# Second attention: output projections and turned maxima in 128x32 column tiles, and the maxima one score chunk earlier in steps with pair sums

## The reference

```
x = conv_attention(x)                     # 1x1 convolutions, softmax over 1024x1024, residual, relu
t = tokens(x)
t = t + attention(layernorm(t))           # 8 heads of 32, the "second attention"
t = t + experts(layernorm(t))             # 8 experts, the best 2 of each token
```

```
qkv = x @ w_qkv
dots = einsum('bhid,bhjd->bhij', q, k) * dim ** -0.5
attn = softmax(dots, axis=-1)
out = einsum('bhij,bhjd->bhid', attn, v)  # then (b, n, 256)
return out @ w_out + b_out
```

## Time and profile before

| what | value |
|---|---|
| three runs | 1159.1, 1163.66, 1166.8 us |
| profiled execution, own time | 1163.12 us |
| its span in the trace | 1161.3 us |
| TensorE clock granted, mean | 0.984 |
| busy: PE, PEld | 1087.0 us (94%), 737.8 us (64%) |
| busy: DVE, ACT, POOL | 816.4, 629.6, 594.3 us |

### The profile page before, as it was taken

The page is one execution under the profiler, slowest core; times in us unless marked ns, Lnnn a source line. Parts: engine busy times, 40 slices in busy tenths (PEclk is TensorE's granted clock), DMA queues, the critical chain, the costliest instruction groups (busy, mean ns, idle before and its releaser), DMA issues.

```text
span 1161.3 us, 34638 instructions
## 1 busy us (share of the span) xinstructions
PE 1087.0 (94%) x13440; PEld 737.8 (64%) x13440; DVE 816.4 (70%) x1489; ACT 629.6 (54%) x1144; POOL 594.3 (51%) x510
## 2 busy tenths in 40 slices
PE   7999998979899998999999989899999999999996
PEld 4464555435455555555555545688898998999884
DVE  4666666666788889788888982777565566565773
ACT  3566675645677667766775665453233333333332
POOL 3425241324588763876487456177554554453530
PEclk9999999998899999999999999999999999999997
DMA  5245851724323231533253213824332332332328
GB/s 177 91 161 202 329 173 60 236 73 154 93 63 94 75 87 35 122 85 103 70 119 93 62 46 101 309 39 92 57 47 47 57 47 48 56 44 41 47 39 294
DMA packets 98908, 121.00 MB, mean 104 GB/s; under 512 B 29024, under 2 KB 76064, under 8 KB 98112
## 3 DMA queue, kind: packets, MB, share of 16 engines
q1 hardware_dynamic: 75280, 70.40, 20.8%
q0 software_dynamic: 20400, 42.08, 15.8%
q10 hardware_dynamic: 3072, 6.30, 1.5%
HBM read 73.10 MB, written 45.47 MB: 102 GB/s over the span
## 4 chain that ended last, share of the span: by engine, by line
PE 70%; DVE 16%; issue 5%; DMA 3%; ACT 2%; DVEq 2%; POOL 1%; SPq 0%; ACTq 0%; POOLq 0%
PE PP L1022 23%; PE PP L1449 13%; DVE mxp L1740 9%; PE PP L1334 7%; PE PP L1306 6%; PE PP L1193 4%; PE PP L1121 4%; PE PP L1253 3%; PE PP L1038 3%; PE PP L1316 2%; PE PP L1321 2%; PE PP L1153 1%; PE PP L1408 1%; DMA res_d<-WORK,lb 1%; DVEq L2019 1%
## 5 line engine op out<-in xcount | busy, mean ns | idle before, releaser
L954 ACT ACTIVATE WB<-PP 128x512 f32<-128x512 f32 x512 | 265.3, 605 | 111.9 <-PE PP L1334 110.7
L1740 DVE TENSOR_REDUCE mxp<-PP 128x2 f32<-128x1024 f32 x242 | 287.0, 1219 | 51.3 <-PE PP L1253 50.7
L992 ACT ACTIVATE WORK<-PP,b1c 128x256 f32<-128x256 f32 (+1 forms) x320 | 139.2, 450 | 234.7 <-PE PP L1022 193.2
L698 POOL TENSOR_TENSOR WB<-WB 128x1024 f32<-128x1024 f32 x81 | 191.7, 2368 | 82.2 <-PE PP L1321 49.6
L781 POOL DMA_INDIRECT res_d<-WORK,lb x70 | 117.1, 1673 | 153.6 <-DVE WORK L2037 136.5
L1449 PE MATMUL PP<-WB,WORK 128*128 x1704 | 193.0, 273 | 0.0
L1022 PE MATMUL PP<-WORK,WB 128*128 128x256 f16 (+1 forms) x1552 | 175.8, 273 | 2.4 <-DVE WORK L2006 1.7
L1449 PEld LDWEIGHTS PP<-WB,WORK 128*128 128x128 f16 x1704 | 164.8, 98 | 19.2 <-issue 0.2
L1022 PE MATMUL PP<-WORK 128*128 128x128 f16 (+6 forms) x1086 | 162.7, 301 | 10.9 <-DVE WORK L1657 3.6
L1022 PEld LDWEIGHTS PP<-WORK,WB 128*128 (+1 forms) x1552 | 152.5, 102 | 21.6 <-issue 4.5
L1334 PE MATMUL PP<-WORK 97*32 97x256 f16 x4096 | 160.0, 276 | 5.0 <-ACT WB L954 4.5
(11 more groups left out here) (318 smaller groups left out, 1197.3 us busy)
## 6 DMA issues: line engine op xcount, KB each, us to landing
WORK<-in_L_ffn_W_dram POOLq DMA_DIRECT2D x32, 512.0 KB, 4.1
res_d<-WORK SPq DMA_DIRECT2D x8, 1024.0 KB, 4.5
late_d<-WB POOLq DMA_DIRECT2D x1, 6144.0 KB, 19.1
WB<-late_d ACTq DMA_DIRECT2D x3, 2048.0 KB, 12.9
v_d<-WORK SPq DMA_DIRECT2D x4, 1024.0 KB, 5.7
WORK<-q_hi_d SPq DMA_DIRECT2D x16, 256.0 KB, 4.0
WORK<-v_d SPq DMA_DIRECT2D x8, 512.0 KB, 5.5
WORK<-k_hi_d SPq DMA_DIRECT2D x16, 256.0 KB, 4.4
```

The source lines that it names most:

```text
L698: pool.tensor_tensor(PS[n % 2], PR[n % 3][:, 0], PR[n % 3][:, 1], ALU.add).then_inc(s("pair_kept"), 1)
L954: act.activation(PR[n % 3][:, c // 2, c % 2 * 2:c % 2 * 2 + 2], SCORES[m % 3] .rearrange("p (h n) -> p h n", h=2), ACT.Exp).then_inc(s("e_ ...
L992: act.activation(hid[:, k, 0:width], hidden_bank(k)[:, 0:width], ACT.Gelu, bias=b1c[:, bass.ds(e, 1), k], scale=1.0 / WSCALE)\
L1740: dve.tensor_reduce(mxp[:, n // 4 % 2, i, h:h + 2, k], PP[2 + h // 2][:, :].rearrange("p (h n) -> p h n", h=2), X_AXIS, ALU.max).then_inc( ...
```

## The change

Three edits. `max_row` uses a plain matmul against the identity where it used a transpose. `tail_project` cuts each of its two products into four, one for every 32 tokens, with the output on the 32 partitions of that tile; it has 8 matmuls of 264 columns where it had 2. In `attend`, a step with pair sums puts the maximum group behind two chunks where it stood behind three; a step with direct sums stays as it was.

```
-                pe.transpose(bank[0:2 * GH, 0:P], mx[:, :], identf[:, :]).then_inc(s("c_made"), 1)
+                pe.matmul(bank[0:2 * GH, 0:P], mx[:, :], identf[:, :], start=True, stop=True).then_inc(s("c_made"), 1)
...
-                tok_at = slice(t * P, (t + 1) * P)
-                product(bank[:, 0:WIDE], [(OS[:, k, tok_at], wo_sb[:, k]) for k in range(CC)], "c_made")
+                for k in range(CC):
+                    for r in range(P // D):
+                        mm = pe.matmul(bank[r * D:(r + 1) * D, 0:WIDE], OS[:, k, t * P + r * D:t * P + (r + 1) * D],
+                                       wo_sb[:, k], start=(k == 0), stop=(k == CC - 1), skip_group_check=True)
+                mm.then_inc(s("c_made"), 1)
...
-                    for c in range(3):
+                    ahead = 3 if direct(n - LAG) else 2
+                    for c in range(ahead):
...
-                    score_chunk(n, 3)
+                    for c in range(ahead, 4):
+                        score_chunk(n, c)
```

## The result

| | before | after |
|---|---|---|
| median of 22 runs each, us | 1162.35 (1158.66 to 1167.68) | 1165.57 (1161.26 to 1169.98) |
| ratio, 95% interval | | 1.0026, 1.0015 to 1.0036 |
| profiled execution, own time, us | 1163.12 | 1164.63 |
| its span, us | 1161.3 | 1162.3 |
| granted clock, mean over the runs | 0.9865 (35 runs beside the first set of experiments) | 0.9825 |

The change costs 3.2 us, and the interval leaves no doubt of the sign. The forecast was 1159.0 (1153 to 1164): wrong in sign and outside the range. It was counted from 1163.66, the median of three runs of before; counted from the 1162.35 of 22 runs, the same 4.7 us would have given 1157.7.

The account below looks back on a forecast made before the run. PE bounds projection steps and DVE's reductions plain pair-sum steps of the second attention. Savings of 1.7 (held group) + 1.8 (last six projections) + 0.7 (turned rows) + 0.5 (transitions) = 4.7 us, from 1163.66 to 1159.0, range 1153 to 1164.

Parts of the forecast that it names:

- The projection in tiles: Second attention: projection falls from 1.08 to 0.89 us, pair sum ahead from 0.54 to 0.43; PE's work 0.30 less per projection.
- Plain steps: Pair-sum steps without a projection, bound by DVE's reductions: stay at 2.86 us from group to group wherever the group stands.
- the group was held: Rival that the group isn't held by DVE: 24 projections save 0.30 us each, 1153.5 us in all; chance 0.14.
- the turned rows do not cost 0.80: Rival that float32 matmul streams 128 columns four times: eight rows lose 4.9 us, 1163.9 us in all; chance 0.04.
- The held group's step: 24 projection steps in batches 1 to 3: PE waits 0.30 us for DVE, step 3.81 against 3.88, saving 1.7 us.
- slower by the held group: Rival that PE waits more than 0.37 us at the group, lengthening projection steps: 1164 to 1167 us; chance 0.06.
- Turned rows: Rows behind direct sums in batches 1 to 3: 0.09 us saved per step, eight times, 0.7 us.
- Behind direct sums [...] PE is the bound: Steps 21, 25, 29 of batches 1 and 2, 21 and 25 of batch 3: PE's time counts, so 0.09 us each.
- Transitions: Where direct sums give way to pair sums, a chunk less between groups: 0.15 us in batches 1 and 2, 0.5 together.
- Six last projections: End of the last batch and behind it, where no groups are left: the full 0.30 us each, 1.8 us.
- next to nothing: Rival that the wait eats the 0.07 and a transfer the end's 1.8 us: 1.2 us remain, 1162.5; chance 0.14.
- The last two: Projections within the first expert tile, between 128x128 products: eight groups of 0.22 plus two switches of 0.11, no change.

Follow-up runs that it names:

- f3: After with the row turned by a transpose again instead of the plain matmul: 1164.12 us, 1.0021 of before.
- h1: Before with only the two projections inside the first expert tile in tiles: 1164.66 us, 1.0014 of before.
- g1: After with three chunks ahead of every maximum group and the last batch's eight projections 128x128 again: 1158.53 us, 0.9967 of before.
- g2: After with three chunks ahead of every maximum group and only the last three projections 128x128 again: 1153.54 us (6 runs), 0.9918 of before.
- h3: The kernel of g2 measured again, in a second set of runs: 1154.44 us (7 runs), 0.9936 of before.
- g4: After with three chunks ahead of the group in the 24 steps behind a projection, two in other pair-sum steps: 1162.63 us, 1.0006 of before.
- e1: After with three chunks ahead of the maximum group in every step, tiles and plain-matmul rows kept: 1159.74 us, 0.9971 of before.

## Why the prediction was wrong, point by point

**Right.** The projection in tiles costs 0.89 us and the pair sum ahead of it 0.43, 0.11 less than ahead of the 128x128 form. These 0.11 us agree with the Trainium skill (TensorEngine Tiling (Array Packing), Key Properties), which says that a change of the tiling mode drains the TensorE; as a rule alone it would have given 0.2 per projection, and 0.30 came. DVE holds the group in all 24 steps. Plain steps stay at 2.86. The transitions out of direct sums gave 0.22 (batch 0) and 0.24 (group 30 of batch 2, forecast 0.24 with its row). Of the rivals, the group was held (so not 1153), and the turned rows do not cost 0.80: two records of 0.27 us lie beside score records, and f3 with a transpose takes the same time. The Trainium skill (TensorE: Matmul & The Clock Gate, Terms) calls float32 four times faster in transpose mode; as time this is not seen here, where the way from the sums to the group is 1.84 us with the plain matmul and 1.94 with the transpose (f3). (Worked out from its own terms, this rival would have cost 8 x (0.80 - 0.22) = 4.6 us and not 4.9.)

**The held group's step: mis-sized, 1.7 forecast, 0.06 measured.** Two small errors lie in it. The group starts 0.89 behind the first chunk and not 0.85: L1785 starts 0.08 behind the end of the last projection record, where before it started 0.04 behind it. (The ends of matmuls are modelled, so that the 0.04 may as well lie in the model.) That made 3.81 into 3.855, 24 x 0.045 = 1.1 us. And 3.88 was taken for all 24 steps of before, from one step in the middle of a run. The first of each run, nine in all, took 3.82: the group ahead of it had waited for DVE and cost 0.33. That is 9 x 0.06 = 0.5 us. The wait's own size was right (24 x 0.28 = 6.8 us).

The rival "slower by the held group" set its limit at 0.37 us of wait. The wait was 0.34 by that count (0.89 - 0.55), so the step stayed just on the winning side.

**Turned rows: 0.7 forecast, about 0.2.** The failed step is "Behind direct sums [...] PE is the bound". Chunk 3 waits there 0.29 us for an exponential, before as after, and takes the 0.11 back. Only the two rows ahead of group 30 paid, and they share their 0.24 with the moved group.

**Transitions: 0.5 forecast, about 0.3.** They gave 0.22 and twice 0.13; missed was group 14, three times 0.05 us longer.

**Six last projections: 1.8 forecast, 0.9 arrived.** The failed step is in the rival "next to nothing": the 1.35 us of idle PE ahead of the turned tokens was looked at as a possible transfer, at 0.14, and dropped. It is a chain of register loads of fixed length, which starts only when PE's sequencer has handed over the matmuls ahead of it. Time won in front of such a chain is won only so far as the sequencer gets there sooner as well.

**The last two "come to about what they cost now: nothing"**, and nothing else behind the hand-over was thought to move. That was the large miss: with tiles the part behind the hand-over is 2.5 to 4.4 us longer. 2 us of it is the clock in both traces of after (0.5 in others), which falls behind a longer idle of PE (2.19 us for 1.35). Most of the rest seems to hang on just the two projections that were booked at nothing (h1: 2.1 us, with an interval that just touches none); by what mechanism is open.

**Sum, from the traces:** 0.06 + 0.2 + 0.3 + 0.9 = 1.5 us won in the attention (1.1 between the traces of before and after; two traces of before differ by 0.7), less 2.5 to 4.4 behind it: 1.0 to 2.9 us slower. The medians say 3.2.

**Open.** Why g1, with all eight whole, is 4 to 5 us above g2 and h3, where the five tiled projections should bring about 1.5; the traces of g1 and g2 themselves (1156.86 and 1157.09 us) don't show the difference. Whether the clock falls at the hand-over seems a matter of chance with a slant: with 2.1 to 2.2 us of idle PE in five traces of six, with 1.2 to 1.4 in two of nine. And what share of the second half the projection right ahead of the loads has, and what share the two behind them.

## What to carry to other kernels

Before a group of work is moved ahead of other work, ask who sets its earliest start. Where another engine sets it and PE is otherwise the bound, each piece that is moved behind it adds its full length (0.22 us here, 24 times), and a cheaper piece ahead of it brings nothing until it has been moved back: do the tiles, leave the order. Take the length of a step from every kind of neighbour it has, not from one in mid-run. And look at what the sequencer has to do behind the last matmul: more and shorter matmuls can cost the lead that hid its register loads. The best version here is three chunks throughout with all projections but the last three in tiles: 1153.5 and 1154.4 us, 0.992 and 0.994 of before.

## What the runs showed of the hardware

- A register load on PE's sequencer follows the one before it at 0.65 us (the second at 0.9 to 1.0), and five with what follows them make 3.6 to 3.7 us in 15 traces. What PE still has to do when they begin hides them only in part: PE idles 1.2 to 1.4 or 2.1 to 2.2 us behind it.
- A float32 product in four 128x32 tiles streams as weighing does (0.22 us for four records of 264 columns), but its result is seen later: DVE starts 0.25 us behind the next matmul's start, 0.11 for the 128x128 form.
- The two float32 records of 8 output rows seem to block one column tile only: three records of the next line start at the same instant as the first of them (462.91).
- The clock fell to its lower level for 3.4 or 6.8 us behind an idle PE of about 2.2 us at the hand-over, at a price of 0.5 and 2.0 us (in g1 and g2 behind one of 1.2 and 1.4 us, in g4 not behind one of 2.2).
- In 16 of the 18 traces (not in e1 and h1) it fell once or twice more at the 20th step of batches 1 to 3, for 3.4 us and at 0.8 to 1.65 us each. PE idles there for DVE's reductions, 1.7 us with three chunks ahead of the group and 1.9 with two. It fell at 11 of the 24 such places with two chunks and at 8 of the 30 with three; that is too few to call the moved group a cause of it.
